# SyncE fetches 19 chunks of source rows one by one, beside the GpSimd gathers of two attention passes

## What is computed

```python
xw = (x @ W).reshape(n, H, D)
a_src = jnp.einsum('nhc,hc->nh', xw, att_src)
a_dst = jnp.einsum('nhc,hc->nh', xw, att_dst)
logits = jax.nn.leaky_relu(a_src[src] + a_dst[dst], NEG_SLOPE)
m = jax.ops.segment_max(logits, dst, num_segments=n)
ex = jnp.exp(logits - m[dst])
s = jax.ops.segment_sum(ex, dst, num_segments=n)
alpha = ex / (s[dst] + EPS)
out = jax.ops.segment_sum(xw[src] * alpha[..., None], dst, num_segments=n)
```

## Time and profile before

| | us |
|---|---|
| median of 3 runs | 7308.85 |
| lowest and highest of them | 7306.36 and 7349.27 |
| the profiled execution | 7287.62 |
| its span | 7285.8 |

### The profile page before, as it was taken

The page is one execution under the profiler, slowest core; times in us unless marked ns, Lnnn a source line. Parts: engine busy times, 40 slices in busy tenths (PEclk is TensorE's granted clock), DMA queues, the critical chain, the costliest instruction groups (busy, mean ns, idle before and its releaser), DMA issues. The chain is left out here.

```text
span 7285.8 us, 87026 instructions
## 1 busy us (share of the span) xinstructions
PE 3973.7 (55%) x21983; PEld 3698.6 (51%) x21983; DVE 3732.6 (51%) x9512; ACT 2921.3 (40%) x5694; POOL 4430.9 (61%) x4701
## 2 busy tenths in 40 slices
PE   4444445454444355555555555545666666666666
PEld 4444444444444344444444444444666666666666
DVE  4333333333333344444444444446777777777777
ACT  2222222222222144444444444444555555555555
POOL 4666666666666556666666666645666666666663
PEclk6555555555555555555555555555555555555555
DMA  5322222222222122222222222222222222222221
GB/s 118 64 52 52 52 52 52 54 52 52 52 52 52 42 54 55 55 55 55 55 55 54 55 55 56 56 55 66 75 74 74 74 74 76 74 74 74 74 74 48
DMA packets 354021, 444.78 MB, mean 61 GB/s; under 512 B 142024, under 2 KB 233574, under 8 KB 353360
## 3 DMA queue, kind: packets, MB, share of 16 engines
q0 software_dynamic: 150112, 217.86, 16.0%
q10 hardware_dynamic: 50400, 132.89, 5.2%
q1 hardware_dynamic: 153424, 93.06, 5.0%
HBM read 407.90 MB, written 39.55 MB: 61 GB/s over the span
## 5 line engine op out<-in xcount | busy, mean ns | idle before, releaser
L1076 POOL DMA_INDIRECT rows<-tab,idx_now x4653 | 4392.7, 944 | 2765.6 <-issue 1631.1
L1383 DVE TENSOR_SCALAR share_prev<-psum,prev_all 128x4 f32<-128x4 f32 x258 | 57.2, 222 | 2253.1 <-remote 2244.9
L2088 PE MATMUL psum<-share,rows 128*65 128x132 f32 (+10 forms) x6240 | 1181.3, 381 | 0.0
L2183 PE MATMUL psum<-own,hot_t 112*128 112x64 f32 x3126 | 697.0, 422 | 859.3 <-DVE mix L1549 734.5
L2183 PEld LDWEIGHTS psum<-own,hot_t 112*128 112x128 f32 x3126 | 674.8, 330 | 887.1 <-issue 646.2
L2088 PEld LDWEIGHTS psum<-share,rows 128*65 128x65 f32 x6240 | 1096.4, 224 | 5.7
L1753 ACT ACTIVATE sums<-psum 65x448 f32<-65x448 f32 x260 | 140.1, 539 | 2053.1 <-remote 2044.0
L2199 PE MATMUL psum<-hot,prob 128*128 128x112 f32 x3126 | 667.8, 406 | 33.4 <-issue 28.8
L2115 PE MATMUL psum<-w_next,turned 65*112 65x72 f32 x262 | 83.4, 421 | 1079.2 <-ACT turned L1757 1079.1
L2199 PEld LDWEIGHTS psum<-hot,prob 128*128 128x128 f32 x3126 | 647.5, 317 | 32.6 <-issue 27.7
L2115 PEld LDWEIGHTS psum<-w_next,turned 65*112 65x112 f32 x262 | 58.0, 281 | 1115.7 <-ACT turned L1757 940.1
(11 more groups left out here) (246 smaller groups left out, 6549.5 us busy)
## 6 DMA issues: line engine op xcount, KB each, us to landing
rel_t<-rel_row ACTq DMA_DIRECT2D x256, 336.0 KB
rows<-tab,idx_now POOLq DMA_INDIRECT x4653
rel_t<-rel_runs ACTq DMA_DIRECT2D x128, 336.0 KB
own<-tab SPq DMA_DIRECT2D x262, 63.0 KB
cut<-cut_row SPq DMA_DIRECT2D x130, 120.2 KB
tab<-row SPq DMA_DIRECT2D x131, 112.0 KB
tab<-row SPq DMA_DIRECT2D x131, 63.0 KB
own<-tab SPq DMA_DIRECT2D x131, 56.0 KB
```

The costliest lines, as they stand in the source:

```text
L1076: nc.gpsimd.indirect_dma_start(rows_of[p][:, G * c.s + j, 0:D] if raw else rows_of[p][:, G * c.s + j, :], None, x if raw else halves[p], b ...
L2088: done = nc.tensor.matmul(summed[:, :, LO[j]:HI[j]], rows_g[:, at + j, 0:D + 1], of[:, j, :, 0:SUBS[j]], start=not opened, stop=j == chunk ...
L2183: done = nc.tensor.matmul(added3[:, j, :], hot_t[k][:, P * j:P * j + P], own3[c.s][:, 0:D], start=True, stop=True)
```

## The change

In passes 0 and 1, 19 chunks are no longer gathered by GpSimd: the 12 of unit 123 and the first 7 of unit 124. They get a place of their own, `side_rows`, laid over the tile `prob3`, which only pass 2 uses. SyncE fetches their 19 x 128 = 2432 rows in each pass, every row by a DMA of its own that moves one piece of 71 numbers to one partition. One chunk is fetched in each of the 19 rounds of the loop. Each unit in the loop thus gets 21 or 22 rows: 10 or 11 of them between the load of `cut` and the store, and 10 or 11 behind the load of `own`. Before each of these two parts SyncE loads the 10 or 11 row numbers from on-chip memory into registers; the numbers themselves come by a small DMA of 64, twice in a round.

```diff
+            def fetch_side_rows(p, c, part):
+                k, done = c.q - 1, (2 * SIDES + 1) * p
+                r0, r1 = [P * (2 * c.s + part + i) // (2 * RING) for i in range(2)]
+                if part == 0 and c.s == 0:
+                    sp.wait_ge(side_src_in, 16 * (2 * c.q - 1 + done))
+                    fetch_side_src(k, 1)
+                if part == 0 and c.s == RING // 2:
+                    sp.wait_ge(side_src_in, 16 * (2 * c.q + done))
+                    fetch_side_src(k + 1, 0)
+                _, nodes = nc.values_load_multi_w_load_instructions(side_src[0:1, r0:r1], engines=(mybir.EngineType.SP,))
+                for r, node in zip(range(r0, r1), nodes):
+                    sp.dma_start(side_rows[r:r + 1, bass.ds(k, 1), 0:SIDE_W].rearrange("p a w -> p (a w)"),
+                                 tab[p][bass.ds(node, 1), HALF:HALF + SIDE_W]).then_inc(side_in[p], 16)
...
                         fetch_cuts(p, c.plus(3))
+                    if aside:
+                        fetch_side_rows(p, c, 0)
...
                             fetch_own(p, c.plus(RING - 1))
+                    if aside:
+                        fetch_side_rows(p, c, 1)
...
-                    for j in range(chunks(c)):
+                    for j in range(beside(c) if p < 2 else 0, chunks(c)):
```

More of the change, by code:

```diff
@@ L105, in build @@
     RAW = 3
+    SIDE, SIDES = NU - 8, (NU - RING) // RING - 1
+    SIDE_W = 71
+    assert G < SIDES < 2 * G and GW <= SIDE_W <= HALF
     SPREADS = [0, RING, 36, 68, 100, NU]
@@ L115, in landed, with came_aside @@
         return 16 * each * c.q + 16 * (before + (tail if c.at_least(NU - 1) else each))
+    def came_aside(p, c, count):
+        return sum(count(m) for before in range(2) for u, m in ((SIDE, G), (SIDE + 1, SIDES - G))
+                   if u % RING == c.s and (before < p or before == p and c.at_least(u)))
     def first_landed(p, c):
-        return landed(p, c, 1, 1, 2, 2)
+        return landed(p, c, 1, 1, 2, 2) - 16 * came_aside(p, c, lambda m: 1)
     def rest_landed(p, c):
-        return landed(p, c, G - 1, LASTC - 1, G - 2, LASTC - 2)
+        return landed(p, c, G - 1, LASTC - 1, G - 2, LASTC - 2) - 16 * came_aside(p, c, lambda m: m - 1)
     def chunks(c):
@@ L413, in build @@
         idx_staged = sem("idx_staged")
+        side_in = [sem(f"side_in{p}") for p in range(2)]
+        side_src_in = sem("side_src_in")
         first_in = [sem(f"first_in{s}") for s in range(RING)]
@@ L508, in build, with beside, chunk_rows @@
         rows_of = (rows_g, rows_g, rows_e)
+        side_rows = prob3[0][:, :, :].rearrange("p c d -> p (c d)")[:, 0:SIDES * HALF].rearrange("p (c w) -> p c w", w=HALF)
+        def beside(c):
+            if not c.at_least(SIDE) or c.at_least(SIDE + 2):
+                return 0
+            return SIDES - G if c.at_least(SIDE + 1) else G
+        def chunk_rows(c, j):
+            if j < beside(c):
+                return side_rows[:, G * (c.u - SIDE) + j, :]
+            return rows_g[:, G * c.s + j, :]
         raw_space = x_tab[0:D, XPART - 8:XPART, :].rearrange("p b c -> p (b c)")
@@ L1009, in _ @@
                 fetch_cuts(p, unit(2))
+                if p > 0:
+                    sp.wait_ge(side_src_in, 16 * p * (2 * SIDES + 1))
+                if p < 2:
+                    fetch_side_src(0, 0)
                 for c in units(sp):
                     n = NU * p + c.u
+                    aside = p < 2 and not isinstance(c.q, int)
                     if p == 1:
@@ L1035, in _ @@
                     sp.wait_ge(row_stored, 32 * NU * (p + 1))
-            sp.wait_ge(dst_copied, 48)
+            sp.wait_ge(dst_copied, 64)
             sp.wait_ge(row_stored, 32 * (NU * 3 - 2))
@@ L1691, in strip_of @@
             def strip_of(p, c):
[L1693 to L1696, removed]
+                n, at, m = NU * p + c.u, G * c.s, chunks(c)
+                heads_of = slice(D + 1, GW)
+                if beside(c.plus(1)) > beside(c):
+                    act.wait_ge(side_in[p], 16 * P * SIDES)
+                if beside(c) < m:
+                    act.wait_ge(rows_in[c.s], rest_landed(p, c))
+                if beside(c) == 0:
+                    act.wait_ge(first_in[c.s], first_landed(p, c))
                 if not (p == 0 and c.below(1)):
@@ L1699, in strip_of @@
                 if not c.below(1):
-                    before = G * c.plus(-1).s + G - 1
-                    nc.scalar.activation(strip[:, 0, :], a_src[:, before, :], ACT.Copy).then_inc(strip_ready, 1)
+                    nc.scalar.activation(strip[:, 0, :], chunk_rows(c.plus(-1), G - 1)[:, heads_of], ACT.Copy)\
+                        .then_inc(strip_ready, 1)
                 else:
                     act.sem_inc(strip_ready, 1)
-                m = chunks(c)
-                nc.scalar.activation(strip[:, 1:m + 1, :], a_src[:, at:at + m, :], ACT.Copy).then_inc(strip_ready, 1)
+                b = beside(c)
+                if b > 0:
+                    first = G * (c.u - SIDE)
+                    copied = nc.scalar.activation(strip[:, 1:b + 1, :], side_rows[:, first:first + b, heads_of], ACT.Copy)
+                if b < m:
+                    copied = nc.scalar.activation(strip[:, b + 1:m + 1, :], rows_g[:, at + b:at + m, heads_of], ACT.Copy)
+                copied.then_inc(strip_ready, 1)
                 if not c.at_least(NU - 1):
-                    act.wait_ge(first_in[c.plus(1).s], first_landed(p, c.plus(1)))
-                    nc.scalar.activation(strip[:, G + 1, :], a_src[:, G * c.plus(1).s, :], ACT.Copy)\
+                    if beside(c.plus(1)) == 0:
+                        act.wait_ge(first_in[c.plus(1).s], first_landed(p, c.plus(1)))
+                    nc.scalar.activation(strip[:, G + 1, :], chunk_rows(c.plus(1), 0)[:, heads_of], ACT.Copy)\
                         .then_inc(strip_ready, 1)
```

28 lines of the change are left out of this document (14 added, 14 removed).

## The result

| | before, us | after, us |
|---|---|---|
| median of 4 runs each | 7308.95 | 9643.61 |
| lowest and highest | 7306.36 and 7349.27 | 9642.78 and 9651.34 |
| span of the profiled execution | 7285.8 | 9641.4 |

The changed kernel takes 1.318 times as long, with a 95% interval from 1.3134 to 1.3226. The forecast was 9000 us and slower.

A forecast was written before the change was run, and what follows sets the result against it. GpSimd, slowed by waits, bounded the kernel; SyncE was to set the pace after the change. 228 units x 7.6 us = 1733 us, less 32, made 8989 profiled and 9010 timed, put at 9000 us; range 7265 to 9750.

The forecast's parts named there:

- The hold: While GpSimd gathers a full set, TensorE's signal of finished sums and SyncE's steps are late until the set is through.
- SyncE's free time: SyncE's true waits at L1019 (942 us) and L982 (153 us) over three passes, taken as 3 to 4 us a unit.
- true waits at L1019 gone: Sign in the changed profile: SyncE, then setting the pace, no longer waits at L1019, where it waited 942 us.
- A unit: Loop unit at SyncE's pace: 12.8 + 10.1 + 1.1 + 0.5 + 1.1 = 25.6 us, 7.6 us more than before.
- The loads of row numbers: SyncE's two loads of row numbers in a loop unit, taken at 0.56 us each, 1.1 us together.
- A row: One row fetch on SyncE, four steps as at L1014, 0.51 us when quiet; 21.3 rows in a loop unit.
- The held stretch: 12.8 us of each loop unit in which SyncE does only 13 slow steps, one and a half rows among them.
- The landing of rows at no cost: Last row is issued in unit 119, three units ahead of its reader; if late, ScalarE waits once in a pass.
- The gathers: 19 fewer gathers a pass: units 123 and 124 run at 10 us instead of 18.04, 32 us saved in both passes.
- Hidden: Rival: SyncE's work of 15 us a unit fits under 18.04, so 7277 us, 0.4% faster; chance 0.25.
- Quick steps, dear loads: Rival: SyncE's steps not slowed, but number loads and longer loop body cost 1 to 4 us a unit, 7500 to 8200 us; chance 0.12.
- Held worse: Rival: number loads cost 0.56 us a number, or hardly any row goes out during a set; above 10700 us; chance 0.07.

The follow-up runs named there:

- The short sets on a held chip: The kernel before with 3 of 12 gathers in the loop units of passes 0 and 1: 5538 us, where the kernel before took 7290.1 us.
- the versions on two queues: Changed kernel with a chunk's rows split between SyncE and ScalarE: 84/44 took 6057.7 us; 96/32 with aligned loads 5946.95 us, then 8732 us on another chip.
- the fifth experiment: The changed kernel itself, unaltered, on a chip where the kernel before took 5978.0 us: 6842.0 us, ratio 1.1443.
- the eleventh: The kernel before with 3 of 12 gathers in the loop units of passes 0 and 1, beside the kernel before at 7290.1 us: 5538 us.

## Why the prediction was right, and where its sizes were off

**The bound and the mechanism: right.** The hold starts about 4.5 us into a set and lasts until it is through; SyncE becomes the engine that sets the pace, with no wait in either loop; VectorE waits for `cut`; GpSimd idles between sets (forecast 10 us, measured 12.4). The short sets on a held chip show that the hold belongs to the set: 7290 us falls to 5538. The changed kernel itself was not run with short sets on a held chip, but the two units in which its gathers are missing or few show the same, below.

**SyncE's free time: misread.** The text took 942 us at L1019 and 153 at L982, spread over three passes, for 3 to 4 us free in each unit. By pass they lie elsewhere. The list of SyncE's waits in the kernel before, first the loop of pass 0 (250 to 2300 us), then pass 2 (4850 us to the end):

```profile
SPq L982 <- DVE row L1450: 52.1, 10, 6.5
SPq L982 <- ACT row L1763: 4.6, 1, 4.6
```

```profile
SPq L1019 <- DVE most L1333: 880.7, 125, 64.8
```

In the loop of pass 1 (2640 to 4690 us) the list is empty. So on the held chip SyncE had 0.5 us free in a unit of pass 0 and nothing in pass 1. The forecast's sum doesn't use that time and stands without it; the sign "true waits at L1019 gone" could not be seen, since the total is 973 us in the changed kernel and lies in pass 2 as before. On a free chip SyncE waits 1308 us in 113 units of pass 0 (11.6 each) and 1170 in 114 of pass 1 (10.3 each) in the kernel with only the gathers gone: that is the room in which rows or loads alone fit, and both together (9.8 + 4.1 us, and the way back) don't.

**A unit: 25.6 us forecast, 27.45 and 29.21 measured.** Three terms make up pass 0.
- The loads of row numbers: forecast 0.56 us each, 1.1 us a unit. A round of six units has four loads of 1.17 us and eight of 2.50, so 24.7 / 6 = 4.1 us a unit. This is the term that failed, by 3.0 us a unit, 684 us in 228 units, more than the 9644 - 9000 that the forecast was short. Its step was to price a load of ten numbers like one of a single number. The other end of the bound, 12 us, was further off. The Trainium skill (Runtime: NRT & Kernel Launch, Instruction fetch mechanics) puts a register load at about 200 ns per register. The estimate by it was 4.3 us a unit, and the trace agrees for loads that begin off a multiple of four (2.50 us for 11); it doesn't for aligned ones, where 12 take 1.01 us. With that estimate the text had 28.8 us a unit and 9740 us, 1% from the result and the nearest of its numbers; that it is so near is partly luck, since a row was counted too dear and pass 1 not apart.
- A row: forecast 0.51 us in four steps, measured 0.46 in three, 1.0 us a unit less. L1014, the row I copied the form from, has a MOVE more. That is also why a round of the loop has 513 steps in the trace and not over 600.
- SyncE's way back to the head of the loop, which was no term: 2.5 us once in six units, 0.4 a unit (the branch at 1480.1, the next step at 1482.6 on the free chip), where the kernel without fetches takes 0.3 (1057.6 and 1057.9). The Trainium skill (same page and section) gives the instruction store of most engines as 512 instructions and says that a taken branch out of its window is a stall. A round of the changed loop has 513 steps in pass 0, one of the kernel without fetches 109, so the trace agrees that the longer body pays a stall that the shorter doesn't. It doesn't show 512 as the border: rounds of 381 and 417 steps, in the versions on two queues on free chips, pay the same 2.5 us. The changed kernel's page also has more on a queue of kind instruction, 271 packets and 2.22 MB where the kernel before has 50 and 0.41 MB. That is 5.8 packets more in each of 38 rounds, and fits a body that is fetched again each time round.

The sum is 25.6 + 3.0 - 1.0 + 0.4 = 28.0 us. The held stretch takes 1.1 off it, as the next point tells: 26.9, against 27.45. The 0.5 us that is left I can't put down to one step. Pass 1 was not priced apart. There SyncE also makes the piece of `rel_runs` in each unit, and a unit is 1.8 us longer.

**The held stretch: right in length, too poor in work.** It runs from 1512.2 to 1524.7 here, 12.5 us of the 12.8 forecast. I had 13 steps in it, as before; it has 25, eight rows and a step. That is a rich one: in 109 sets of the loop of pass 0, 22 steps and 7.2 DMAs of rows begin between 4.3 us after the set's start and 2.3 us after the end of its last gather. A held step takes 0.7 us or a few ns, and those of rows are more often the short kind than those of the store and of `own`. The store and `own` fall outside, which costs 1.5 us at quiet prices, and at the mean 5.7 rows more than forecast fall inside, which saves 5.7 x 0.46 = 2.6: together 1.1 us less.

**The landing of rows at no cost: ScalarE did wait, and the total shows nothing of it.** The argument was that the last row is issued in unit 119 and read three units later. But the other engines run ahead of SyncE. When they reach the end of the loop they wait for it (the row of SyncE is of its own timeline, 11 row fetches from 3393.71 on):

```profile
3368.31 0.52 ACT L1814 ACTIVATE sums<-psum 65x448 f32<-65x448 f32 x1
...
3393.71 4.86 SPq L1032 DMA_DIRECT2D prob<-tab  x11
...
3399.54 0.21 ACT L1755 ACTIVATE strip<-rows 128x4 f32<-128x4 f32 x1 [30.45 <-DMA prob<-tab]
...
3407.91 0.54 ACT L1814 ACTIVATE sums<-psum 65x448 f32<-65x448 f32 x1 [1.51 <-PE psum L2148]
```

The step from unit 120 to 121 is 39.6 us in pass 0 and 49.4 in pass 1, where a unit there is 18. "If rows landed late, ScalarE would wait once in a pass" was in the text; so it was, though not because rows land late: ScalarE goes on 1 us after the last is issued. Nor is it a cost on top. In the first three or four units of the loop the others ran ahead and no unit was longer than before, while SyncE already fell behind; the wait pays that back, and 114 units at the mean pace make 2353 of the 2356 us. The sum of the forecast, 228 units at SyncE's pace, lacked no term here. The text of the fifth experiment added 65 us for it, and came out 48 us too high.

**The gathers: 32 us forecast.** Alone they gave 37.5 us, on a free chip; alone on a held chip they were not run. In the changed kernel on the held chip little of it is seen: from the sums of unit 121 to those of unit 130 pass 0 takes 114.9 us (111.9 before) and pass 1 takes 113.1 (117.1 before). But it is there earlier, at SyncE's pace. GpSimd has no set between 3316.4 and 3347.2, and one of 5 gathers until 3353.2. SyncE is not held in that gap, as its fetches from 3319 to 3347 show:

```profile
L1032 SPq MOVE prob<-tab x32: 29/29/29, 3322.8 to 3344.6; - x32
```

The sums of units 119 and 120 follow after 17.7 and 20.1 us, where a unit is 27.5: 17 us less in pass 0, and as much in pass 1 (20.4 and 20.9 where it is 29.3). So the size, 2 x 8 us a pass, was right, and the stretch wrong: the two units of 10 us that were named as a sign are not there, since SyncE, not the other engines, sets their length.

**The rivals.** "Hidden" (7277 us) falls on a held chip, and on a free one too, where the changed kernel is 14% slower: SyncE's quiet unit is 18.1 us, not 15, with the loads and the way back, and GpSimd's unit is 15.0, not 18.04. "Quick steps, dear loads" describes the free chip well: the steps are not held, and loads and rows together cost more than SyncE has to spare. Its 7500 to 8200 us were added to the 7309 of a held chip, though; the free chip took 6842, 864 more than the kernel before, within the 228 to 912 that it gave. "Held worse" falls: rows go out in the held stretch.

**What stays open:** why one chip holds its engines while GpSimd gathers and another doesn't. The job of the fifth experiment and that of the eleventh carry the same chip number and differ in it. What is held isn't settled either: signals, steps of SyncE and the start of work on three engines all stop together.

## What to carry over

Read the waits of a queue engine in the stretch that is to take more work, not over the whole program: here they lay in another pass. Then price its unit step by step, the loads of registers and the way back of the loop included, and compare the sum with the pace of the engine that leads. Load numbers into registers from places in a tile that are multiples of 16 bytes, which took 524 us off here for a change of borders. If the time before isn't the same on all chips, find out which engine waits on which chip before a gain of half a per cent is trusted: the same kernel was 0.65% faster on one chip and 20% slower on the next.

## What the runs showed of the hardware

- A load of consecutive numbers into registers, on SyncE: from a multiple of 16 bytes in the tile 0.77 us for 8, 1.01 for 12, 1.17 for 10 (two over a multiple of four cost more than four do); from elsewhere 1.89 for 8, 2.29 for 10 and 2.51 for 11. On ScalarE an aligned load of 4 took 0.49 us.
- On a held chip SyncE's steps come in ticks of 0.7 us from 4 to 5 us after the start of a set of 12 gathers (in the changed kernel 3.5 at the earliest, in the version on two queues 0.6) until it is through. TensorE, VectorE and ScalarE start nothing from 1011 to 1017, around the end of a set that ran from 1001.45 to 1016.12, and go on after it. A set of 3 gathers (3.4 us) costs little: 9.24 us a unit against 8.54 on a free chip. On a free chip no row fetch is held, in 4864 of them.
- The way back to the head of a loop took SyncE 2.5 us where a round of the body has 513, 417 or 381 steps, and 0.3 where it has 109.
